# A hybrid attention stack on one core: what stays in the step, what moves behind it, and a centring in two rounded products

## The chip, the cores and the metric

The kernel runs on one core of one Trainium2 chip. The metric is device time in microseconds, the median of three runs of the same program. PE is TensorE, DVE is VectorE, ACT is ScalarE, POOL is GpSimd, SP is SyncE. PSUM is read by DVE and ACT and written by PE; POOL works on SBUF alone.

## The reference

The input x has 4 sequences of 512 tokens and 128 features. Four blocks follow each other, each with a residual:

```
x = x + attention_a(layernorm(x))          # 16 heads of 8, softmax, dense
x = x + ffn(layernorm(x))                  # two layers, below
x = x + attention_b(layernorm(x))          # linear attention, elu + 1
x = x + ffn(layernorm(x))                  # the same weights again
ffn layer: h = shift_token(x); q, k, v = h @ wqkv     # 8 heads of 64
           q, k = rotary_xpos(l2norm(q) * qs, l2norm(k) * ks)
           x = x + local_attention(q, k, v) @ wo      # windows of 64, one back
           h = layernorm(shift_token(x)) * lg + lb
           a, g = split(h @ w1 + b1); x = x + (a * gelu(g)) @ w2 + b2
```

`shift_token` delays the upper 64 features by one token. In the kernel's layout, features on partitions and tokens along the row, that is a copy of partitions 64 to 127 by one column. All is float32; large products are made from a value rounded to FP32R (`_h`, the high part) and what the rounding left (`_l`, the low part).

## The kernel before, in words

The program has two phases, `attention_a` and `stream`, both written with semaphores by hand. The change lies in `stream`. It walks over 64 tiles of 128 tokens: 2 calls of the ffn, 2 layers each, 4 sequences, 4 tiles to a sequence. Four tiles are a group (16 of them): what is done for a whole sequence is done once in a group.

Each engine has a list in `STEP` (L985): a stage, a lag in steps, and whose turn it is. In step s an engine runs the stages of its list in the order in which they stand there, each for tile s minus its lag. So an engine's order is fixed, and an instruction that waits holds up all that stands behind it. `of_tile` stages run in every step, `of_group` stages in every fourth, and `of_sequence` stages once for each sequence between the two calls, where attention b and two layer norms lie. Counting from the last tile of a group, the output product `wo` comes at lag 3, the MLP's centring at 4, `w1` at 5, `w2` at 6 on PE and its result on DVE at 7. So steps come in fours. I name them by their group work: step A has `wo` (and on DVE the result of the group before, `w2`), step B the MLP's centring and its variance, step C `w1` and the gelu, step D `w2`. Of a sequence between the calls, A has the norm b (`center_b`, `var_b`), B the latent and key products, C the context and token products, D the projection and the norm y (`center_y`, `var_y`).

In every step PE turns the weighed scores (`turn_p`, L1314), projects q, k and v (L1265 to L1267), turns q and k (L1276), multiplies by the values (`sums`, L1324), and makes the next scores (L1289, L1304). ACT squares and copies, takes the row norms (`norm`) and the exponentials (`soften`, L1499). DVE copies the turned scores (`PT`, L1644), sums and inverts them (`weigh`, L1661, L1663), does the rotary products (`rope`, L1616, L1620, L1627) and the maxima (`soften`, L1652). POOL multiplies the scores by the inverse sums (`weigh`, L1196), adds the rotary halves and scales them by the row norms (`scale`, L1185, L1190).

PSUM has 8 banks and PE takes them in turn: `take` gives the product number x bank x modulo 8, and waits until what read the product 8 before has gone through (`FREED`). So every bank that is read late stops PE, though the data of the product itself are there.

A layer norm has a product that takes off the mean (`center_*`, L1366), a square on ACT (L1537), a product with ones (`var_*`, L1372), Ln and Exp on ACT (L1544, L1547), and DVE's multiplication (stage `var_*`, L1676 to L1692). For the MLP (`center_mlp`) POOL first makes the shifted sequence in `mid` (stage `wo`, L1216 to L1220), and PE multiplies it in float32. After `w2`, DVE writes the high part `HH` of the next layer's input straight from PSUM in two halves (L1717) and then `Y` (L1721); POOL makes the low part `HL` (L1177, stage `w2`). Norm y does the same on DVE (L1689, L1692) and POOL (stage `var_y`). Layer 1 of a call has no such parts: there DVE writes only X (L1710), and POOL adds Y to X behind `mid` (L1224).

Of the kernel before, what the change touches and what calls it, by code (L numbers as in the profile page):

```python
# [7 lines left out]
F32 = mybir.dt.float32  # L8
# [971 lines left out]
def of_first(k):  # L980
# [5 lines left out]
    "PE": [("turn_p", 3, of_tile), ("turn_p_2", 3, of_tile),  # L986
# [4 lines left out]
           ("center_y", 10, of_sequence), ("keys_b", 8, of_sequence), ("tokens_b", 9, of_sequence), ("scores", 1, of_tile),  # L991
           ("var_mlp", 4, of_group), ("var_a", 3, of_first), ("var_b", 7, of_sequence),
           ("var_y", 10, of_sequence), ("w2", 6, of_group), ("wo", 3, of_group), ("store", 7, of_end)],
    "ACT": [("squares", 0, of_tile), ("latent", 8, of_sequence), ("features_b", 10, of_sequence), ("values", 0, of_tile),
            ("turn", 1, of_tile), ("sums", 3, of_tile), ("features_a", 1, of_first),
            ("center_mlp", 4, of_group), ("center_a", 3, of_first), ("center_b", 7, of_sequence),
            ("center_y", 10, of_sequence), ("split", SEQS, of_tile), ("w1", 5, of_group), ("keys_b", 8, of_sequence),
            ("norm", 0, of_tile), ("var_mlp", 4, of_group), ("var_a", 3, of_first), ("var_b", 7, of_sequence),
            ("var_y", 10, of_sequence), ("soften", 1, of_tile), ("split_w1", 4, of_first), ("store", 7, of_end)],
    "DVE": [("lead", 0, of_lead), ("turn_p", 3, of_tile), ("var_mlp", 5, of_group), ("var_a", 4, of_first),  # L1000
            ("var_b", 8, of_sequence), ("var_y", 11, of_sequence), ("w2", 7, of_group),
            ("weigh", 2, of_tile), ("latent", 8, of_sequence), ("rope", 0, of_tile),
            ("project_a", 2, of_first), ("context", 9, of_sequence), ("project_b", 10, of_sequence),
            ("w1", 5, of_group), ("keys_b", 8, of_sequence), ("soften", 1, of_tile),
            ("tokens_b", 9, of_sequence), ("wo", 3, of_group)],
    "POOL": [("split_w1", 5, of_first), ("lead", 0, of_lead), ("split", SEQS, of_tile), ("weigh", 2, of_tile), ("scale", 0, of_tile), ("w2", 6, of_group),
             ("wo", 3, of_group), ("latent", 8, of_sequence), ("var_y", 10, of_sequence)],
# [32 lines left out]
def stream(nc, a, g, out):  # L1040
# [53 lines left out]
    with ExitStack() as ctx:  # L1094
# [21 lines left out]
        mid = sb("mid", [P, T])  # L1116
# [16 lines left out]
        OF = g.raw[:, 2 * T:3 * T]  # L1133
# [5 lines left out]
        with block:  # L1139
# [25 lines left out]
            def _(pool):  # L1165
# [6 lines left out]
                nc.gpsimd.memset(mid[64:P, 0:1], 0.0).then_inc(s("mid_zero"), 1)  # L1172
                pool.wait_ge(s("mid_zero"), 1)
# [7 lines left out]
                for stage, i in engine_plan("POOL"):  # L1181
# [29 lines left out]
                    elif stage == "wo":  # L1211
# [4 lines left out]
                        nc.gpsimd.tensor_copy(mid[0:64, :], Y[0:64, n, :]).then_inc(s("shifted_mid"), 1)  # L1216
                        pool.wait_ge(s("shifted_mid"), 2 * i + 1)
                        nc.gpsimd.tensor_copy(mid[64:P, 1:T], Y[64:P, n, 0:T - 1]).then_inc(s("shifted_mid"), 1)
                        if i:
                            nc.gpsimd.memset(mid[64:P, 0:1], 0.0).then_inc(s("mid_zero"), 1)  # L1220
                            pool.wait_ge(s("mid_zero"), i + 1)
                        pool.wait_ge(s("shifted_mid"), 2 * i + 2)
# [3 lines left out]
                    elif stage == "w2" and not last_layer(i):  # L1226
                        pool.wait_ge(s("y_new"), i + 1)
                        call = i // (SEQS * LAYERS)
                        low_part(i % SEQS, "shifted", 2 * (SEQS * call + i % SEQS))
                    elif stage == "latent":  # L1230
                        pool.wait_ge(s("q_exp"), i + 1)
                        pool.wait_ge(s("q_pos"), i + 1)
                        nc.gpsimd.tensor_tensor(QB[:, :], QB[:, :], NEG[:, :], ALU.add).then_inc(s("q_ready"), 1)
                    elif stage == "var_y":
                        n = i
                        pool.wait_ge(s("ln_used"), number["y", n] + 1)
                        low_part(n, "again_shifted", 2 * n)

            @block.tensor
            def _(pe):  # L1240
# [89 lines left out]
                for stage, i in engine_plan("PE"):  # L1330
# [20 lines left out]
                    elif stage[:7] == "center_":  # L1351
                        use, j = stage[7:], i
                        if use == "mlp":
                            pe.wait_ge(s("shifted_mid"), 2 * j + 2)
                            pe.wait_ge(s("mid_zero"), j + 1)
                            x = mid[:, :]
# [9 lines left out]
                        nc.tensor.matmul(take("center", number[use, j]), cst("center"), x, start=True, stop=True)\  # L1366
                          .then_inc(s("center"), 1)
# [73 lines left out]
                    elif stage == "project_a":  # L1441
                        pe.wait_ge(s("o_ready_a"), 1)
                        nc.tensor.matmul(take("project_a", i), g.wpa[:, :], NEG[:, :], start=True, stop=True)\
# [13 lines left out]
            def _(act):  # L1457
                for stage, i in engine_plan("ACT"):
# [102 lines left out]
                    elif stage == "split_w1":  # L1561
                        nc.scalar.activation(w1_h[:, :, :], w1, ACT.Copy).then_inc(s("w1_high"), 1)
                    elif stage == "latent":
# [3 lines left out]
                        else:  # L1567
                            act.wait_ge(s("ones_b"), 2)
                        nc.scalar.activation(LAT[0:32, :], psum[0:32, bank("latent", i), :], ACT.Identity,
                                             bias=g.bd_b[:, 0:1]).then_inc(s("latent_ready"), 1)  # L1570
                        act.wait_ge(s("q_neg"), i + 1)
# [28 lines left out]
            def _(dve):  # L1600
# [6 lines left out]
                for stage, i in engine_plan("DVE"):  # L1607
# [61 lines left out]
                    elif stage[:4] == "var_":  # L1669
# [4 lines left out]
                        if use == "mlp":  # L1674
# [126 lines left out]
```

## Time and profile before

| | us |
|---|---|
| median of 3 runs | 1014.11 (1013.69 to 1014.61) |
| the profiled execution | 1009.97 |
| its span, first to last instruction | 1007.9 |
| PE busy | 916.4 (91%) |
| DVE busy | 796.0 (79%) |
| ACT busy | 701.6 (70%) |
| POOL busy | 509.8 (51%) |

The span begins with attention a; the stream's first scores come at some 257 us and its last store at the end. Busy PE is not PE at its peak, since the ends of matmuls are modelled, so waits of PE are read from the timeline, where the number in brackets is the idle time just before an instruction and what ended it.

### The profile page before, as it was taken

How to read it: one execution, taken by the hardware profiler on the slowest of the kernel's cores; microseconds unless marked ns; L12 is line 12 of the kernel's file. 1: busy time of each engine (PE TensorE's matmuls, PEld its weight loads, DVE VectorE, ACT ScalarE, POOL GpSimd, SP SyncE). 2: the span in 40 equal slices, each digit the busy share in tenths (PEclk: the TensorE clock that was granted, in tenths of full speed). 3: DMA queues.
4: the chain of work that ended last, by engine and by line, in shares of the span. 5: the costliest groups of instructions: out<-in, count | busy, mean ns of one | idle time of the engine just before them, and what ended most of it. 6: DMA issues, size and time to landing. Idle time of an engine off the chain costs nothing.

```text
span 1007.9 us, 22385 instructions
## 1 busy us (share of the span) xinstructions
PE 916.4 (91%) x8584; PEld 569.8 (57%) x8584; DVE 796.0 (79%) x1170; ACT 701.6 (70%) x1500; POOL 509.8 (51%) x336
## 2 busy tenths in 40 slices
PE   8999999999778999999988887888979999999985
PEld 4333333333556776776756564565747677677753
DVE  6887878885678899999977687756778999998862
ACT  3577777778576696887866575665758688787753
POOL 2110113123577668578664545544456857867730
PEclk9999999999989999999999999999999999999997
DMA  2211000000201001101000000000000110101100
GB/s 81 65 39 33 2 1 2 3 1 2 70 16 28 22 17 33 29 17 33 18 22 17 12 17 22 17 12 16 12 23 17 33 28 17 33 17 38 35 10 21
DMA packets 23205, 23.46 MB, mean 23 GB/s; under 512 B 8530, under 2 KB 14972, under 8 KB 23100
## 3 DMA queue, kind: packets, MB, share of 16 engines
q1 hardware_dynamic: 23100, 22.04, 8.8%
q8 instruction: 69, 1.13, 0.5%
q14 instruction: 36, 0.29, 0.1%
HBM read 6.16 MB, written 1.05 MB: 7 GB/s over the span
## 4 chain that ended last, share of the span: by engine, by line
PE 50%; DVE 14%; issue 5%; POOL 3%; ACT 3%; DVEq 0%; ACTq 0%; POOLq 0%
PE psum L1348 5%; PE psum L1324 5%; PE psum L1304 5%; PE psum L1392 4%; PE psum L1276 4%; PE psum L1314 3%; PE psum L1265 3%; DVE f_PT L1644 3%; PE psum L1366 3%; PE psum L1383 2%; PE psum L1267 2%; PE psum L1266 2%; PE psum L1384 2%; PE psum L1385 2%; PE psum L1372 2%
## 5 line engine op out<-in xcount | busy, mean ns | idle before, releaser
L876 DVE TENSOR_REDUCE a_M<-psum 128x2 f32<-128x1024 f32 x128 | 155.3, 1220 | 33.4 <-PE psum L650 32.7
L1196 POOL TENSOR_TENSOR f_PW<-f_PW,f_RD 128x1024 f32<-128x1024 f32 x64 | 121.4, 1898 | 102.9 <-DVE f_RD L1663 101.1
L1185 POOL TENSOR_TENSOR A<-A,BS 128x1024 f32<-128x1024 f32 x62 | 146.8, 2368 | 33.2 <-DVE BS L1620 33.2
L1190 POOL TENSOR_TENSOR A<-A,RN 128x1024 f32<-128x1024 f32 x62 | 118.1, 1905 | 64.3 <-ACT RN L1514 58.7
L773 ACT ACTIVATE a_PT<-psum 128x1024 f32<-128x1024 f32 x128 | 128.9, 1020 | 23.8 <-PE psum L660 23.7
L1499 ACT ACTIVATE f_PW<-psum,f_NM 128x128 f32<-128x128 f32 x512 | 138.4, 380 | 5.6 <-DVE f_NM L1652 5.5
L1652 DVE TENSOR_REDUCE f_NM<-psum 128x4 f32<-128x512 f32 x128 | 82.1, 683 | 43.3 <-PE psum L1304 43.3
L1644 DVE COPY f_PT<-psum 128x512 f32<-128x512 f32 x128 | 82.3, 683 | 29.0 <-PE psum L1314 28.9
L1465 ACT ACTIVATE SQ<-psum 128x512 f32<-128x512 f32 x124 | 72.5, 622 | 39.5 <-PE psum L1267 35.7
L1661 DVE TENSOR_REDUCE f_RD<-f_PW 128x8 f32<-128x1024 f32 x64 | 77.5, 1211 | 9.4 <-ACT f_PW L1499 9.4
L1620 DVE TENSOR_TENSOR BS<-psum,sin 128x512 f32<-128x512 f32 x124 | 84.2, 679 | 0.0
L1616 DVE TENSOR_TENSOR A<-psum,cos 128x512 f32<-128x512 f32 x124 | 82.7, 667 | 0.0
L571 PE MATMUL psum<-a_PT,a_VA 128*12 128x256 f32 x1024 | 79.6, 383 | 0.6 <-ACT a_PT L773 0.6
L1314 PEld LDWEIGHTS psum<-const,f_PW 128*128 128x128 f32 x512 | 59.2, 142 | 34.2 <-issue 24.4
L1314 PE MATMUL psum<-const,f_PW 128*128 128x128 f32 x512 | 68.7, 278 | 7.0 <-POOL f_PW L1196 7.0
L1627 DVE TENSOR_REDUCE SS<-SQ 128x16 f32<-128x1024 f32 x62 | 74.8, 1207 | 0.0
L1276 PE MATMUL psum<-const,A 128*128 128x128 f32 x512 | 68.0, 276 | 6.7 <-POOL A L1190 4.7
L1304 PE MATMUL psum<-f_KT,f_QT 64*64 64x128 f32 x2048 | 70.5, 278 | 2.9 <-ACT f_KT L1489 2.9
L1324 PE MATMUL psum<-f_PT,f_VS 128*64 128x64 f32 x1024 | 67.0, 229 | 4.5 <-DVE f_PT L1644 2.7
L1276 PEld LDWEIGHTS psum<-const,A 128*128 128x128 f32 x512 | 59.1, 142 | 20.3 <-POOL A L1190 10.7
L1304 PEld LDWEIGHTS psum<-f_KT,f_QT 64*64 64x64 f32 x2048 | 61.9, 138 | 10.8 <-ACT f_KT L1489 6.8
L1324 PE MATMUL psum<-f_PT,V 128*64 128x64 f32 x1024 | 64.1, 223 | 0.0
(216 smaller groups left out, 2007.5 us busy)
## 6 DMA issues: line engine op xcount, KB each, us to landing
f_VS<-V SPq DMA_DIRECT2D x112, 128.0 KB, 2.3
raw<-L_ffn_wqkv_dram SPq DMA_DIRECT2D x2, 768.0 KB, 4.6
a_XT<-L_attn_a_x_dram SPq DMA_DIRECT2D x4, 256.0 KB, 2.8
out_dram<-raw SPq DMA_DIRECT2D x4, 256.0 KB, 2.3
gates<-L_ffn_w_dram SPq DMA_DIRECT2D x2, 341.0 KB
tables<-const_dram SPq DMA_DIRECT2D x1, 512.0 KB, 3.8
wo<-L_ffn_wo_dram SPq DMA_DIRECT2D x2, 256.0 KB
const<-const_dram SPq DMA_DIRECT2D x1, 264.0 KB, 3.1
```

The costliest lines, as they stand in the source:

```text
L773: nc.scalar.activation(PT[:, i % 4, :, :], psum[:, pair("by_key", i), :], ACT.Exp, scale=float(DA) ** -0.5).then_inc(s("exped"), 1)
L876: nc.vector.tensor_reduce(M[:, quads % 2, t, 2 * j:2 * j + 2], psum[:, pair("scores", i), :], AX_X, ALU.max).then_inc(s("maxed"), 1)
L1185: nc.gpsimd.tensor_tensor(A[:, k % 2, :, :], A[:, k % 2, :, :], BS[:, k % 2, :, :], ALU.add)\
L1190: nc.gpsimd.tensor_tensor(x, x, RN[:, k % 2, :, None].to_broadcast([P, 2 * HW, DW]), ALU.mult)\
L1196: nc.gpsimd.tensor_tensor(x, x, RD[:, k % 2, :, None].to_broadcast([P, 2 * PAIRS, P]), ALU.mult)\
L1276: last = nc.tensor.transpose(dst[:, P * c:P * c + P], A[:, k % 2, w, P * c:P * c + P], g.ident)
L1304: last = nc.tensor.matmul(dst[j][WIN * w:WIN * w + WIN, P * c:P * c + P].rearrange("p (s x) -> p s x", s=2), QT[rows, k % 2, c, WIN * w:WI ...
L1314: last = nc.tensor.transpose(dst[:, P * c:P * c + P], PW[:, u % 4, c, :], g.ident)
L1324: last = nc.tensor.matmul(dst[DW * j:DW * j + DW, c, WIN * w:WIN * w + WIN], values[:, k % 4, 2 * c + j, :], PT[:, (2 * k + j) % 4, c, WIN ...
L1499: last = nc.scalar.activation(PW[:, u % 4, c, :], psum[:, bank("scores", u), P * c:P * c + P], ACT.Exp, bias=NM[:, u % 4, c:c + 1])
L1620: nc.vector.tensor_tensor(BS[:, k % 2, w, :].rearrange("p (h s d) -> p h s d", s=2, d=DW // 2), x.rearrange("p (h s d) -> p h s d", s=2, d ...
L1644: nc.vector.tensor_copy(PT[:, u % 4, :, :], psum[:, bank("turn_p", u), :].rearrange("p (c x) -> p c x", c=PAIRS))\
```

## The change

All of it is in `stream`.

- Order. PE: `center_y` goes from ahead of the scores to behind `w2`, at the end of step D; `var_y` goes from the end of step D into the next step (A), behind the two `turn_p`. ACT: the squares and roots of norm y move likewise; the exponential of attention b's queries becomes a stage of its own (`latent_exp`) behind `w1`. DVE: the stages `var_mlp` and `var_b`, which stood at the head of the next step, go to the end of the step in which the variance is made, ahead of `wo`; what frees no bank there is split off: `rest_mlp` (L1680, L1683) stays in step C behind `turn_p`, and `rest_w2` and `rest_y` copy HH from Y in SBUF, behind `rope` and behind `soften`. `latent` goes behind `rope`. POOL: `weigh` and `scale` now stand first; `split`, `split_w1` and `lead` last; the low part after `w2` is made at lag 7 (step A, ahead of the stage `wo`) and not at lag 6 (step D); that of norm y at lag 11.
- The MLP's centring. POOL makes the high and the low part of the shifted sequence, and PE multiplies each by a rounded centring matrix `centre`, in place of one float32 product of `mid`.
- A buffer: OF of its own, which attention a's last features use too.

```diff
 "PE":
-  ("turn_p", 3), ("turn_p_2", 3), ("project", 0) ...
+  ("turn_p", 3), ("turn_p_2", 3), ("var_y", 11), ("project", 0) ...
-  ("center_b", 7), ("center_y", 10), ("keys_b", 8) ... ("var_b", 7), ("var_y", 10), ("w2", 6), ("wo", 3)
+  ("center_b", 7), ("keys_b", 8) ... ("var_b", 7), ("w2", 6), ("center_y", 10), ("wo", 3)
 "ACT":
+  ("var_y", 11) first; ("latent_exp", 8) behind ("w1", 5); ("center_y", 10) just ahead of ("soften", 1)
 "DVE":
-  lead, turn_p 3, var_mlp 5, var_a 4, var_b 8, var_y 11, w2 7, weigh, latent 8, rope,
-  project_a, context 9, project_b 10, w1, keys_b 8, soften, tokens_b 9, wo 3
+  lead, turn_p 3, var_y 11, rest_mlp 5, w2 7, weigh, rope, rest_w2 7,
+  project_a, context 9, project_b 10, latent 8, w1, keys_b 8, soften, rest_y 11,
+  tokens_b 9, var_mlp 4, var_a 3, var_b 7, wo 3
 "POOL":
-  split_w1 5, lead, split, weigh 2, scale 0, w2 6, wo 3, latent 8, var_y 10
+  weigh 2, scale 0, w2 7, wo 3, latent 8, var_y 11, lead, split_w1 5, split
```
```diff
 POOL, stage wo:
-  tensor_copy(mid[0:64, :], Y[0:64, n, :])
-  tensor_copy(mid[64:P, 1:T], Y[64:P, n, 0:T - 1])
-  memset(mid[64:P, 0:1], 0.0)
+  for half, (rows, to, of) in enumerate(SHIFTED):
+      tensor_copy(mid_h[rows, to], Y[rows, n, of])
+  tensor_copy(mid_h[64:P, 0:1], HH[64:P, n, 0:1]); tensor_copy(mid_l[64:P, 0:1], HL[64:P, n, 0:1])
+  for half, (rows, to, of) in enumerate(SHIFTED):
+      tensor_tensor(mid_l[rows, to], Y[rows, n, of], mid_h[rows, to], subtract)
 PE, center_mlp:
-  matmul(dst, cst("center"), mid, start=True, stop=True)
+  matmul(dst, centre, mid_h, start=True, stop=False); matmul(dst, centre, mid_l, start=False, stop=True)
 DVE, w2 of layer 0:
-  for rows, to, of in SHIFTED: scalar_tensor_tensor(out=HH[rows, n, to], in0=psum ..., in1=Y ...)
   scalar_tensor_tensor(out=Y[:, n, :], in0=psum ..., in1=Y[:, n, :])
+ DVE, rest_w2 (and rest_y alike):
+  for rows, to, of in SHIFTED: tensor_copy(HH[rows, n, to], Y[rows, n, of])
 POOL, stage w2:
-  pool.wait_ge(s("y_new"), i + 1)
+  pool.wait_ge(s("high"), ...)       # rest_w2's two copies
```

## Rows read from the trace of the kernel before

**Rows 1.** Busy time by stretch: length, then engines with instructions, granted clock, DMA share, GB/s.

```profile
421.65:460.74 39.09, 38.39 (x410) 27.65 (x409) 36.09 (x54) 30.63 (x77) 28.17 (x18) 1.00 0.11 25
558.26:618.93 60.67, 51.71 (x451) 34.45 (x450) 43.22 (x70) 37.95 (x90) 30.76 (x19) 0.97 0.07 16
601.47:618.93 17.46, 14.42 (x113) 8.64 (x110) 10.99 (x20) 9.49 (x27) 8.05 (x4) 0.90 0.07 16
612.07:615.48 3.41, 3.41 (x39) 1.90 (x37) 0.00 (x0) 1.31 (x4) 0.92 (x2) 0.50 0.02 5
726.08:741.96 15.88, 12.85 (x113) 7.80 (x110) 10.99 (x20) 9.47 (x27) 8.05 (x4) 1.00 0.08 18
```

**Rows 2.** Timeline, PE in sequences: start, length, line, idle time before and its releaser.

```profile
611.54 0.73 PE L1366 MATMUL psum<-X,const 128*128 128x512 f32 x1 [2.97 <-DVE X L1778]
622.96 0.50 PE L1265 MATMUL psum<-w_h,HH 128*128 128x512 f32 x1 [2.29 <-DVE Y L1692]
635.90 0.50 PE L1265 MATMUL psum<-w_h,HH 128*128 128x512 f32 x1 [1.00 <-DVE Y L1692]
642.39 1.10 PE L1366 MATMUL psum<-f_mid,const 128*128 128x512 f32 x2 [0.83 <-DVE BS L1620]
650.38 0.48 PE L1265 MATMUL psum<-w_h,HH 128*128 128x512 f32 x1 [1.69 <-DVE f_ln_squared L1676]
```

**Rows 3.** Timeline of a layer-0 group: PE, DVE and POOL from step A on.

```profile
421.65 1.04 PE L1314 MATMUL psum<-const,f_PW 128*128 128x128 f32 x8
423.49 1.52 DVE L1717 SCALAR_TENSOR_TENSOR HH<-psum,vecs,Y 64x512 fp32r<-64x512 f32 x2
428.47 3.67 PE L1348 MATMUL psum<-f_OT,wo 128*128 128x512 f32 x8 [0.21 <-DVE BS L1620]
428.84 0.68 DVE L1620 TENSOR_TENSOR BS<-psum,sin 128x512 f32<-128x512 f32 x1
435.81 0.10 POOL L1220 MEMSET f_mid<- 64x1 f32 x1
436.98 1.13 PE L1366 MATMUL psum<-f_mid,const 128*128 128x512 f32 x2
443.65 1.03 PE L1276 MATMUL psum<-const,A 128*128 128x128 f32 x8
```

**Rows 4.** Groups by line and form, POOL: busy us, mean ns of one, idle before.

```profile
L1185 POOL TENSOR_TENSOR A<-A,BS 128x1024 f32<-128x1024 f32 x62 | 146.8, 2368 | 33.2 <-DVE BS L1620 33.2
L1196 POOL TENSOR_TENSOR f_PW<-f_PW,f_RD 128x1024 f32<-128x1024 f32 x64 | 121.4, 1898 | 102.9 <-DVE f_RD L1663 101.1
L1190 POOL TENSOR_TENSOR A<-A,RN 128x1024 f32<-128x1024 f32 x62 | 118.1, 1905 | 64.3 <-ACT RN L1514 58.7
L1177 POOL TENSOR_TENSOR HL<-Y,HH 64x512 fp32r<-64x512 f32 x13 | 16.6, 1274 | 42.4 <-DVE Y L1721 22.3 <-DVE Y L1692 19.2 <-DVE HH L1604 0.8
L1177 POOL TENSOR_TENSOR HL<-Y,HH 64x511 fp32r<-64x511 f32 x13 | 14.2, 1089 | 1.0
L1218 POOL COPY f_mid<-Y 64x511 f32<-64x511 f32 x16 | 9.8, 612 | 1.0
```

**Rows 5.** The chain in order of time: start, us, what; PE's issue of one product.

```profile
437.05 1.05 PE psum L1366 x2
446.19 0.23 PE psum L1384
```

**Rows 6.** DVE's SBUF copies at L1604 (min/median/max ns), and POOL then.

```profile
L1604 DVE CAST HH<-Y x2: 425/1240/2056, 319.5 to 321.5; 64x512 fp32r<-64x512 f32 x1, 64x511 fp32r<-64x511 f32 x1
319.33 1.91 POOL L1190 TENSOR_TENSOR A<-A,RN 128x1024 f32<-128x1024 f32 x1
```

**Rows 7.** The stream's start: POOL's weight split ahead of weighing, and DVE.

```profile
302.19 0.20 DVE L1663 RECIPROCAL f_RD<-f_RD 128x8 f32<-128x8 f32 x1
306.17 1.26 POOL L1209 TENSOR_TENSOR f_qkv_l<-raw,f_qkv_h 128x512 fp32r<-128x512 f32 x1 [3.53 <-ACT f_qkv_h L1528]
```

**Rows 8.** The last group: PE's wait for the shifted sequence.

```profile
986.72 1.10 PE L1366 MATMUL psum<-f_mid,const 128*128 128x512 f32 x2 [1.77 <-POOL f_mid L1218]
```

More of the change, by code:

```diff
@@ L998 @@
             ("norm", 0, of_tile), ("var_mlp", 4, of_group), ("var_a", 3, of_first), ("var_b", 7, of_sequence),
[L999 to L1005, printed above, removed]
@@ L1006 @@
-    "POOL": [("split_w1", 5, of_first), ("lead", 0, of_lead), ("split", SEQS, of_tile), ("weigh", 2, of_tile), ("scale", 0, of_tile), ("w2", 6, of_group),
-             ("wo", 3, of_group), ("latent", 8, of_sequence), ("var_y", 10, of_sequence)],
+            ("center_y", 10, of_sequence), ("soften", 1, of_tile), ("split_w1", 4, of_first), ("store", 7, of_end)],
+    "DVE": [("lead", 0, of_lead), ("turn_p", 3, of_tile), ("var_y", 11, of_sequence), ("rest_mlp", 5, of_group),
+            ("w2", 7, of_group), ("weigh", 2, of_tile), ("rope", 0, of_tile), ("rest_w2", 7, of_group),
+            ("project_a", 2, of_first), ("context", 9, of_sequence), ("project_b", 10, of_sequence), ("latent", 8, of_sequence),
+            ("w1", 5, of_group), ("keys_b", 8, of_sequence), ("soften", 1, of_tile), ("rest_y", 11, of_sequence),
+            ("tokens_b", 9, of_sequence), ("var_mlp", 4, of_group), ("var_a", 3, of_first),
+            ("var_b", 7, of_sequence), ("wo", 3, of_group)],
@@ L1008 @@
+    "POOL": [("weigh", 2, of_tile), ("scale", 0, of_tile), ("w2", 7, of_group),
+             ("wo", 3, of_group), ("latent", 8, of_sequence), ("var_y", 11, of_sequence), ("lead", 0, of_lead), ("split_w1", 5, of_first), ("split", SEQS, of_tile)],
     "SP": [("values", 0, of_tile), ("store", 7, of_end)],
@@ L1115, in stream @@
         w1_l = sb("w1_l", [P, LAYERS, 2 * HID], F32R)
-        mid = sb("mid", [P, T])
+        centre = sb("centre", [P, P], F32R)
         mid_h = sb("mid_h", [P, T], F32R)
@@ L1132, in stream @@
         OB = sb("OB", [P, 4, HA, DA])
-        OF = g.raw[:, 2 * T:3 * T]
+        OF = sb("OF", [P, T])
         OUT = g.raw[:, 0:8 * P].rearrange("p (b t d) -> p b t d", b=2, t=4)
@@ L1442, in _ @@
                         pe.wait_ge(s("o_ready_a"), 1)
-                        nc.tensor.matmul(take("project_a", i), g.wpa[:, :], NEG[:, :], start=True, stop=True)\
+                        nc.tensor.matmul(take("project_a", i), g.wpa[:, :], OF[:, :], start=True, stop=True)\
                           .then_inc(s("project_a"), 1)
@@ L1723, in _ @@
                               .then_inc(s("y_new"), 1)
+                    elif stage == "rest_w2":
+                        if not last_layer(i):
+                            dve.wait_ge(s("y_new"), i + 1)
+                            for rows, to, of in SHIFTED:
+                                nc.vector.tensor_copy(HH[rows, i % SEQS, to], Y[rows, i % SEQS, of])\
+                                  .then_inc(s("high"), 1)
                     elif stage == "latent":
```

83 lines of the change are left out of this document (44 added, 39 removed).

## The prediction

> **What bounds the kernel now.** The page's slices show PE at eight or nine tenths all through, so I looked first for where PE is not busy, by stretches [rows 1]. Two kinds of steps stand out. A layer-0 group, four steps without work of the sequences, takes 39.09 us, of which PE is busy 38.39 and DVE 36.09; POOL has 28.17. There PE is the bound, with DVE close behind, and less than 1 us of waiting is to be had. Four steps in which a sequence passes between the calls take 60.67, of which PE is busy 51.71: 9 us of waiting in each. There are four sequences. Step D alone takes 17.46 with 14.42 of PE.
>
> The timeline says what PE waits for in such four steps [rows 2]: 2.97 us for X, ahead of `center_y` in D; 2.29 for Y in A, because the bank of that centring comes free only when DVE has made two halves of HH and then Y; 1.00 in B for the Y of norm b; 0.83 in B at the MLP's centring, for a bank that `rope` frees late; 1.69 in C for the bank of the MLP's centring. That is 8.8 of the 9. All are of one kind: an instruction in PE's or DVE's fixed order stands ahead of others that could run. The granted clock adds to the first: for 3.41 us behind the wait it is 0.50, the 1.2 GHz level, and a D without such a stretch takes 15.88, not 17.46 [rows 1].
>
> **Norm y and the sequences: 32 us off.** In D, X is ready at 611.5. Behind the scores and `w2`, PE comes to `center_y` later than that, so the 2.97 goes, and with it the half clock, some 1.6. Against that, the scores must now wait for `rope` to free their second bank, about 1.2 us after PE gets there, and `var_y` (about 1, as one float32 product of 512 columns) goes to A. I get 13.1 for D, 4.4 off in the three that show the low clock, 2.8 in the fourth: 16. In A, Y needs no HH ahead of it any more, so the 2.29 goes; but ACT's square now waits for the late `center_y` and holds up the exponentials behind it, so Ln and Exp of norm y come about 4 us into A, and the result of `w2` behind Y at 5.7, where PE wants its bank at 3.9. With `var_y` itself A stays at 14.2 to 14.4: 0, and 1 off for the one A that had a low clock. In B, the 1.00 and the 0.83 go, since `var_b` stands ahead of `wo` and `latent` behind `rope`; with 0.5 of the cheaper centring and what the earlier `rope` frees I take 2.9 in each, 12 to 13. In C, the MLP's multiplication now stands ahead of the copies PT, which takes 0.6 of the 1.69. Four times that is 2.4. The sum is 16 + 1 + 12.6 + 2.4 = 32. From below, if only D gains, it is 16; from above, all of the 8.8, the clock and the cheaper centring, it is 4 x 11 = 44. I take 32, since each term goes by a named wait.
>
> **The start: 5 us off.** In each of three steps POOL waits for ACT's rounding of a weight block and only then weighs: the inverse sums were ready at 302.4, the split ran from 306.17 to 307.4, and weighing began behind it [rows 7]. Behind `scale`, the split delays nobody in its own step, but it and `split_w1` push the next step's weighing. Following the three steps through, PE's turn in step 8 comes 5 us earlier. The bounds are the three splits alone, 3 x 1.26 = 3.8, and three times this wait of 5.0, 15.
>
> **The MLP's centring: dearer on POOL than it is cheaper on PE.** On PE a float32 product of 512 columns is two passes, 1.05 with the last; an FP32R product issues in 0.23 [rows 5]. Two of those for 1.05 save about 0.5. On POOL `mid` was two copies and a memset, 1.3. Now there are two rounding copies (0.6 each), two of one column (0.1 each, as the memset [rows 3]) and two subtractions like those of HL (1.27 and 1.09 [rows 4]): 3.8, and with six waits on its own results 4.1. So 2.8 more in each of 16 groups, and PE waits for it. Whether that shows depends on where POOL stands, so I follow one layer-0 group from A's first transposition, 421.65 [rows 3].
>
> In A, HH's two halves (1.5) leave DVE ahead of `weigh`, so `rope` ends its last product not at 7.9 but at 6.4. PE's `wo`, which waited for it, comes 0.56 earlier, and with it the unhindered centring of B: 436.98 - 421.65 - 0.56 = 14.8. POOL, though, has a row of work that no longer has a gap. It adds the halves from 6.45 on: 2.37, then 0.15 and 1.9 for the scaling, to 10.9 [rows 4]. Then comes the low part after `w2`, which used to run in the wait at the step's head and now stands between: 2.43, to 13.4, or to 13.9 since HH's copies come late (below). Then the parts of the shifted sequence, 4.1, to 17.5 or 18.0. So PE waits 3 us at the centring, where it waited for nothing. From 18.0 POOL goes on with B's weighing, addition and scaling, 1.9 + 2.37 + 1.9 and 0.25 between, to 24.4, and C's turn of q and k needs that. It stood at 443.65 - 421.65 = 22.0. The group ends 2.4 later than before, in spite of the cheaper centring and of A's 0.56.
>
> There are five such groups, 12. In the two where the new group is of layer 1, POOL's addition to X (1.28) lies in the chain too: 3.5 each, 7. In the step where the last sequence's norm y meets this, both low parts are in the chain: 3. In two groups of layer 1 without HL I get 0.8 each, 1.6. In the sequences' steps PE has the latent products ahead of the centring, and POOL comes in time: 0. The sum is 24. From below it is 0, if POOL's work can hide after all; from above the whole 2.8 + 2.43 in each of ten, 52. I take 24, since the chain is the sum of durations that hardly vary.
>
> At the end nothing hides it: PE waits 1.77 for the shifted sequence even now [rows 8], so the last group costs 2.8 - 0.5 = 2.3 more. A PE that waits 3 us may run at 1.2 GHz for a stretch, as in D; there that cost 1.6 in three of four cases. Here most of it lies beside POOL's chain; I add 2.5 in all, from bounds of 0 and 8 x 1.6 = 13.
>
> **The copies of HH.** They read SBUF now and no longer PSUM. Where POOL stood still such a copy took 0.43; the one that met POOL's scaling, which began 0.13 before it, took 2.06 and ended behind it [rows 6]. So `rest_w2`, which comes just while POOL adds and scales, costs DVE between 0.85 and some 4 us. In a layer-0 group DVE then waits beside POOL, and PE waits longer for POOL in any case: 0 to 0.5, in the 18.0 above.
> The Trainium skill (SBUF — State Buffer, Who interferes with whom) has a rule that speaks against this move: the port pair that VectorE and GpSimd share is an exclusive lock, held for a whole instruction by whichever starts first, for copies in a two-port mode too. The row agrees for one direction. By the rule DVE can also come first, and then POOL's chain grows by up to 0.85 in each group with a low part: that would make 1013 of the time, and it is in the second rival.
>
> **The sum.** The terms are -32 - 5 + 24 + 2.3 + 2.5 = -8.2. The profiled execution's 1009.97 becomes 1001.8. The median of the runs lies 4.1 above that execution, and I carry that over: 1014.1 - 8.2 = 1005.9, so 1006. The other edits, OF's buffer, `project_a`, the rounding of `centre`, are single instructions beside other work: 0.
>
> **The rivals.**
> 1. POOL's chain is hidden: PE's order or DVE's delays leave POOL the time, and its 24 + 2.5 fall to some 5. Then 1014.1 - 32 - 5 + 2.3 + 5 = 984; with half of it, 995. For it: POOL is busy only 28 of 39 us in a group [rows 1]. Against it: its work is in the middle, and both ends of the chain are fixed.
> 2. POOL's chain is dearer, and the kernel slower. Place: step A and B of the eight groups where a low part comes ahead of the centring. Price: 2.4 to 3.5, and 1.6 for the clock, and 0.85 where DVE's copies go first: 5 to 6 in each, 45 in all. It decides from 4.4 in each, where 8 x 4.4 + 2.3 is the 37 that the rest saves. At 45 the time is 1014.1 - 37 + 45 + 2.3 = 1024. For it: a wait of 2.97 already brings the low clock.
> 3. The sequences gain in D alone: the waits in A, B and C come back under other names, since DVE is busy 43.2 of 60.67 and its order has few gaps. Then 1014.1 - 16 - 5 + 26.5 + 2.3 = 1022. Against it: each of those waits has its own cause, which the change takes away.
> 4. Gain and loss even out: 1014.
>
> **How the numbers follow.** What tells two runs of this kernel apart is about 0.2%, 2 us. My forecast, 1006 with its own range of 998 to 1012, has 0.48. Rival 1 has 0.22, rival 2 0.13, rival 3 0.08, rival 4 0.09. Faster is the forecast and rival 1, 0.70; the same is rival 4, 0.09; slower is rivals 2 and 3, 0.21. The range of 8 in 10 takes in half of rival 1 and the near ends of the slower ones: 989 to 1020.
>
> **What would show it.** Right: in the changed kernel's timeline PE waits 2 to 3 us for POOL's subtraction at the MLP's centring in layer-0 groups, and a group takes 41 to 42 us; step D takes 13 and B 11 to 12; four steps of a sequence take 52 to 54. POOL's work in a group [rows 1] rises by 2.8. Wrong: groups of 39 us or less (rival 1), a clock of 0.5 in each group (rival 2), or sequences of 57 and more (rival 3).

## The result and the profile after: slower by 0.9%, since the centring now waits for two engines

| | before | after |
|---|---|---|
| median of five runs, us | 1014.11 (1009.55 to 1014.87) | 1022.64 (1020.00 to 1023.77) |
| ratio to before | | 1.0088 [1.0061, 1.0114] |
| profiled execution; its span | 1009.97; 1007.9 | 1022.71; 1020.7 |
| PE, DVE, ACT, POOL busy in the span | 916.4, 796.0, 701.6, 509.8 | 923.1, 816.6, 696.4, 553.7 |

The page of the changed kernel, the busy time of each engine:

```profile
span 1020.7 us, 22419 instructions
PE 923.1 (90%) x8584; PEld 572.4 (56%) x8584; DVE 816.6 (80%) x1170; ACT 696.4 (68%) x1501; POOL 553.7 (54%) x384
```

The page names no culprit: POOL has 44 us more to do, DVE 21, PE 7. Where the time went is seen by steps, numbered as in `STEP`: step 3 is the first in which PE turns weighed scores, and step 18 the A of the layer-0 group below. The table takes the start of each step from PE's first transposition of the weighed scores and adds up the lengths of the steps. It compares one profiled execution of each kernel.

| stretch | before | after | difference | forecast |
|---|---|---|---|---|
| up to step 9 (the start) | 343.4 | 340.7 | -2.7 | -5 |
| steps 10 to 25, four groups in which POOL makes HL | 156.9 | 173.5 | +16.6 | |
| steps 26 to 41, the four sequences | 241.6 | 212.2 | -29.4 | -32 |
| steps 42 to 57, four more of them | 161.3 | 179.9 | +18.6 | |
| steps 58 to 65, two groups without HL | 73.6 | 78.7 | +5.2 | |
| all groups together | 391.8 | 432.2 | +40.4 | +24 +2.5 |
| from step 66 to the end | | | +4.5 | +2.3 |

The windows of the changed kernel that answer to rows 1: two layer-0 groups that follow each other (with and without a stretch at half clock), that stretch, a step D, a sequence's four steps (columns as there).

```profile
384.51:428.26 43.75, 40.46 (x409) 28.32 (x408) 38.21 (x54) 30.14 (x77) 30.89 (x21) 0.96 0.10 22
428.26:470.47 42.21, 38.98 (x410) 27.38 (x409) 38.21 (x54) 30.14 (x77) 30.95 (x21) 1.00 0.10 23
403.70:407.11 3.41, 3.41 (x32) 1.94 (x25) 1.29 (x2) 0.90 (x4) 3.27 (x3) 0.50 0.00 0
605.79:618.94 13.15, 11.79 (x111) 7.57 (x108) 10.90 (x20) 6.65 (x19) 8.05 (x4) 1.00 0.09 21
565.07:618.94 53.87, 49.48 (x451) 33.79 (x450) 44.53 (x70) 37.70 (x89) 33.65 (x22) 1.00 0.08 18
```

A sequence now takes 53.87 and not 60.67, at the full clock throughout. But a layer-0 group takes 42.21 or 43.75 and not 39.09. Eight groups have POOL's HL ahead of the centring as these two do; in two of them POOL also adds to X, and in one the last sequence's norm y comes in. The timeline of the group without half clock, where A begins at 428.26 and B at 438.01 (start, length, line; in brackets the idle time before and its releaser):

```profile
434.65 2.35 POOL L1183 TENSOR_TENSOR A<-A,BS 128x1024 f32<-128x1024 f32 x1 [0.47 <-DVE BS L1630]
435.62 3.71 DVE L1733 CAST HH<-Y 64x512 fp32r<-64x512 f32 x2
437.14 1.90 POOL L1188 TENSOR_TENSOR A<-A,RN 128x1024 f32<-128x1024 f32 x1
439.41 2.46 POOL L1175 TENSOR_TENSOR HL<-Y,HH 64x512 fp32r<-64x512 f32 x2 [0.36 <-DVE HH L1733]
440.68 0.69 DVE L1677 TENSOR_TENSOR Y<-Y,psum 128x512 f32<-128x512 f32 x1
441.94 1.28 POOL L1215 CAST f_mid_h<-Y 64x512 fp32r<-64x512 f32 x2
443.79 2.43 POOL L1222 TENSOR_TENSOR f_mid_l<-Y,f_mid_h 64x512 fp32r<-64x512 f32 x2
446.32 0.47 PE L1371 MATMUL psum<-f_mid_h,f_centre 128*128 128x512 f32 x1 [2.27 <-issue]
452.61 1.09 PE L1278 MATMUL psum<-const,A 128*128 128x128 f32 x8
```

Read it from the last but one line upwards. PE waits 2.27 us at the centring; the profile writes "issue", but POOL's second subtraction ends at 446.22, 0.1 before. POOL goes from 437.14 to there almost without a gap: the scaling, HL, the two casts, two copies of one column, the two subtractions. And DVE stands in its own copies of HH for 3.71 us, beside POOL's addition and scaling; the maxima come only behind them, and then Y (L1677), from which POOL makes the centring's parts (the high and the low part of the shifted sequence).

The first three of these lines are step C of the same group: two lines of DVE stand in a new order, and PE waits for a bank behind them. The fourth is the last group, where PE's wait of rows 8 has grown by 2.96:

```profile
450.71 0.75 DVE L1686 SCALAR_TENSOR_TENSOR f_ln_squared<-psum,vecs,f_LR 128x512 f32<-128x512 f32 x1 [1.11 <-ACT f_LR L1555]
451.38 1.28 DVE L1654 COPY f_PT<-psum 128x512 f32<-128x512 f32 x2
457.63 0.50 PE L1391 MATMUL psum<-f_mid_h,f_w_h 128*128 128x512 f32 x1 [0.23 <-DVE BS L1630]
997.94 0.76 PE L1371 MATMUL psum<-f_mid_h,f_centre 128*128 128x512 f32 x1 [4.73 <-issue]
```

PE's waits of the changed kernel, by line (total, times, longest); the second is the one that rows 2 show with 1.69 in step C of a sequence:

```profile
PE psum L1371 <- issue: 21.8, 9, 4.7
PE psum L1267 <- DVE f_ln_squared L1686: 5.8, 4, 1.4
PE psum L1391 <- DVE BS L1630: 4.8, 17, 0.8
```

### The profile page after: what moved, and what is told of

Its sections match the earlier page's. It is cut to its first block, busy times and chain, and to the rows that moved or that the text cites. A ratio compares the mean times of both kernels' runs of the same rounds, so it can differ in the third digit from the quotient of the medians.

```text
span 1020.7 us, 22419 instructions
## 1 busy us (share of the span) xinstructions
PE 923.1 (90%) x8584; PEld 572.4 (56%) x8584; DVE 816.6 (80%) x1170; ACT 696.4 (68%) x1501; POOL 553.7 (54%) x384
## 4 chain that ended last, share of the span: by engine, by line
PE 37%; DVE 15%; ACT 8%; issue 7%; POOL 6%; DVEq 0%; ACTq 0%; POOLq 0%
PE psum L1306 5%; PE psum L1400 4%; ACT f_PW L1507 4%; PE psum L1326 4%; PE psum L1278 3%; DVE BS L1630 3%; PE psum L1316 2%; PE psum L1380 2%; DVE A L1626 2%; DVE HH L1733 2%; PE psum L1391 2%; DVE f_RD L1671 2%; PE psum L1350 2%; PE psum L1291 2%; POOL A L1183 2%
## 5 line engine op out<-in xcount | busy, mean ns | idle before, releaser
L773 ACT ACTIVATE a_PT<-psum 128x1024 f32<-128x1024 f32 x128 | 129.0, 1020 | 23.9 <-PE psum L660 23.7
L1188 POOL TENSOR_TENSOR A<-A,RN 128x1024 f32<-128x1024 f32 x62 | 118.0, 1903 | 43.5 <-ACT RN L1522 36.2
L1662 DVE TENSOR_REDUCE f_NM<-psum 128x4 f32<-128x512 f32 x128 | 82.2, 684 | 35.5 <-PE psum L1306 35.2
L1278 PE MATMUL psum<-const,A 128*128 128x128 f32 x512 | 70.1, 277 | 23.3 <-POOL A L1188 10.5
L1278 PEld LDWEIGHTS psum<-const,A 128*128 128x128 f32 x512 | 56.7, 140 | 43.9 <-POOL A L1188 18.6
L1473 ACT ACTIVATE SQ<-psum 128x512 f32<-128x512 f32 x124 | 71.5, 631 | 11.1 <-PE psum L1269 9.1
L1306 PE MATMUL psum<-f_KT,f_QT 64*64 64x128 f32 x2048 | 74.3, 288 | 2.5 <-ACT f_KT L1497 2.5
L1306 PEld LDWEIGHTS psum<-f_KT,f_QT 64*64 64x64 f32 x2048 | 65.1, 144 | 10.6 <-ACT f_KT L1497 6.5
```

Of the source, the lines that this page charges most:

```text
L773: nc.scalar.activation(PT[:, i % 4, :, :], psum[:, pair("by_key", i), :], ACT.Exp, scale=float(DA) ** -0.5).then_inc(s("exped"), 1)
L1188: nc.gpsimd.tensor_tensor(x, x, RN[:, k % 2, :, None].to_broadcast([P, 2 * HW, DW]), ALU.mult)\
L1278: last = nc.tensor.transpose(dst[:, P * c:P * c + P], A[:, k % 2, w, P * c:P * c + P], g.ident)
L1306: last = nc.tensor.matmul(dst[j][WIN * w:WIN * w + WIN, P * c:P * c + P].rearrange("p (s x) -> p s x", s=2), QT[rows, k % 2, c, WIN * w:WI ...
```

## The experiments

The theory after the comparison: the order gains what it was forecast to gain; the split centring loses it again, because in each group its parts end later than PE comes to it. I call a gate what must be done before the centring can begin. Rivals: the order itself costs the groups their time (VectorE's blocked copies, its moved `var_mlp`); or the half clock behind the wait does. All are variants of the changed kernel, but `split_only`, which is one of the kernel before. The stretches are those of the table by steps, in us of the profiled execution; B and C are medians of steps 10 to 25. Each ratio is to runs of the kernel before from the same round. The edits are shown shortened.

| run | ratio to before [95%] | 10-25 | 26-41 | 42-57 | 58-65 | B | C |
|---|---|---|---|---|---|---|---|
| before | 1 | 156.9 | 241.6 | 161.3 | 73.6 | 8.24 | 11.17 |
| after | 1.0088 [1.0061, 1.0114] | 173.5 | 212.2 | 179.9 | 78.7 | 12.62 | 11.99 |
| order_only | 0.9797 [0.9752, 0.9842] | 164.5 | 213.1 | 169.6 | 75.1 | 9.39 | 12.61 |
| split_only | 1.0425 [1.0372, 1.0477] | 168.4 | 252.3 | 171.0 | 79.9 | 10.57 | 11.72 |
| low_later | 1.0009 [0.9983, 1.0036] | 169.2 | 212.2 | 174.7 | 78.8 | 10.80 | 12.04 |
| filler | 1.0028 [1.0007, 1.0049] | 170.1 | 212.2 | 176.2 | 78.7 | 11.14 | 12.02 |
| act_copies | 1.0085 [1.0051, 1.0119] | 171.5 | 212.2 | 180.5 | 77.3 | 11.96 | 12.03 |
| both_gates | 0.9797 [0.9762, 0.9833] | 158.4 | 212.2 | 164.2 | 78.8 | 8.19 | 12.01 |
| var_head | 1.0066 [1.0046, 1.0087] | 171.3 | 212.7 | 177.3 | 78.8 | 12.44 | 11.60 |
| order_var_head | 0.9792 [0.9735, 0.9849] | 161.0 | 214.1 | 166.5 | 73.6 | 9.39 | 11.72 |
| all_three | 0.9802 [0.9776, 0.9829] | 157.6 | 212.6 | 164.2 | 78.7 | 8.18 | 11.80 |
| order_var_act | 0.9647 [0.9621, 0.9673] | 155.9 | 214.2 | 161.5 | 73.6 | 8.24 | 11.29 |

### The two halves of the change

`order_only`: the new order; the centring, and the buffer of OF, as before.

```diff
 POOL, stage wo:
-  mid_h: two rounding copies and one column; mid_l: one column and two subtractions
+  mid: two copies and a memset
 PE, center_mlp:
-  matmul(dst, centre, mid_h, stop=False); matmul(dst, centre, mid_l, start=False)
+  matmul(dst, cst("center"), mid)
```

> The changed order of the engines with the float32 centring of before (POOL makes mid in two copies and a memset); OF and the last features of attention a are as before. Theory: in the changed kernel POOL's low part and the four copies and two subtractions of the centring stand in one chain ahead of it, which ends 17.96 us after step A begins. Without the subtractions it ends at 13.9 + 1.3 = 15.2, PE's centring comes at 14.8, so PE waits 0.5 and not 2.3 to 2.5, its clock stays up, and step B takes 8.5 to 9 and not 12.6: some 3.7 off in each of eight groups, the end 4 off, the sequences 2 longer: about 988 us. Step C stays near 12.0 if DVE's order sets it, and falls to 11.2 if POOL's chain sets it. Rival, the order itself loses (HH copied in SBUF blocks DVE for 3.7 us, the MLP's multiplication stands ahead of PT): B stays over 11 and the time over 1012.

Measured: 992.19 us; B is 9.39, more than the 8.5 to 9 expected, and C 12.61, over the 12.0 expected if DVE's order sets it. `split_only` is the other half, the same lines with the signs turned round, in the kernel before:

> The kernel before with the centring in two products alone. Theory: POOL's scaling in step A ends 13.0 us after the step's start, the parts take 4.3, so the centring waits from 15.3 to 17.3; weighing, adding and scaling behind it bring C's turn of q and k to 23.8 where it was 22.0. A group takes 1.8 longer, 3.3 with a low clock, with POOL's addition to X 1.3 more; eight to eleven groups and the end (2.3): 1030 to 1045 us. Rival, the order is what loses: the two products save 0.5 a group, and the time is at most 1014.

Measured: 1055.24 us, beyond the 1030 to 1045 expected, since the sequences lose too. So the order alone is worth 2.0%, and the split centring alone costs 4.2% in the old order and, from 0.9797 to 1.0088, 2.9% in the new one, some 29 us. It has not been a gain in either. In the old order the sequences take longer by it (252.3 for 241.6); in the new order they do not (212.2 with the split, 213.1 without). But `order_only` is not free of loss either: its four groups take 164.5 where the kernel before has 156.9. B has 1.1 too much, C 1.4. In B, with no wait at the centring, the same copies of HH stand ahead of the maxima as in the changed kernel:

```profile
426.87 3.71 DVE L1724 CAST HH<-Y 64x512 fp32r<-64x512 f32 x2
430.61 1.29 DVE L1653 TENSOR_REDUCE f_NM<-psum 128x4 f32<-128x512 f32 x2
432.63 0.63 PE L1276 MATMUL psum<-const,A 128*128 128x128 f32 x4 [0.24 <-ACT f_PW L1499]
433.57 0.66 PE L1276 MATMUL psum<-const,A 128*128 128x128 f32 x4 [0.31 <-ACT f_PW L1499]
```

### What the wait's half clock costs

`filler`: PE is given two float32 products ahead of the wait, whose result is overwritten, in the eight groups.

```diff
 PE, center_mlp, in eight groups:
+  for _ in range(2): matmul(dst, cst("ones"), cos)
   pe.wait_ge(s("mid_high"), 3 * j + 3)
```

> The changed kernel; in eight groups PE makes two more float32 products of 512 columns into the centring's own bank (the centring overwrites them) where it would wait for POOL, so that it stands still for 0.5 us and not 2.3. If the low clock behind the wait costs time of its own, B falls from 12.6 to 11.1 in the seven groups that show 0.50, and the time to about 1012. If the clock's part lies beside POOL's chain, as the prediction put it, the time stays at 1020 to 1023 or rises.

Measured: 1015.39 us. Timeline of PE at the centring, and the window of the group:

```profile
443.95 1.98 PE L1371 MATMUL psum<-cos,const 128*128 128x512 f32 x4
446.33 0.47 PE L1376 MATMUL psum<-f_mid_h,f_centre 128*128 128x512 f32 x1 [0.40 <-POOL f_mid_l L1222]
```
```profile
428.24:470.52 42.28, 40.96 (x413) 28.05 (x412) 38.19 (x54) 30.12 (x77) 30.95 (x21) 1.00 0.10 23
```

The centring comes 18.09 us into A, as in the changed kernel (18.06), but the granted clock stays at 1.00, in all eight groups, where it fell to 0.50 in seven. The medians differ by 7.3 us, and steps 10 to 57 are 7.1 shorter. So work that is thrown away bought 7 us. In four groups B is 1.4 to 1.5 shorter than in the changed kernel and C is not longer for it (11.99 and 12.02): there the half clock was not hidden beside POOL's chain. In the two groups in which POOL also adds to X it was hidden for the larger part: B is 1.2 and 1.3 shorter, but C 0.7 and 1.0 longer, and PE waits for POOL there, in the changed kernel not:

```profile
496.15 1.09 PE L1278 MATMUL psum<-const,A 128*128 128x128 f32 x8 [1.22 <-POOL A L1188]
```

### What holds the centring's parts

`low_later`: HL leaves POOL's chain, two steps later.

```diff
 "POOL":
-  ("weigh", 2), ("scale", 0), ("w2", 7) ...
+  ("weigh", 2), ("scale", 0), ("w2", 9) ...
```

> The changed kernel with one lag: POOL makes the low part after w2 at lag 9 (step C), and no longer ahead of the centring's parts in step A. Theory: the parts end at 11.0 + 4.3 = 15.3 us into A and B, PE waits 0.5, no low clock, B takes 8 to 8.5 and not 12.6; the low part fits into C's wait of POOL. Eight groups times 4: about 992 us. Rival, DVE is held by the copies of HH (3.7 us beside POOL, unchanged here) or by its new order: B stays at 11 or more, the time over 1012.

Measured: 1012.64 us; far from what was expected, since PE's wait only went from 2.27 to 1.78. The half clock came in three of the eight groups, though PE's wait was 1.77 or 1.78 in seven of them alike. Timeline, A from 425.83:

```profile
433.19 3.71 DVE L1733 CAST HH<-Y 64x512 fp32r<-64x512 f32 x2
438.25 0.69 DVE L1677 TENSOR_TENSOR Y<-Y,psum 128x512 f32<-128x512 f32 x1
439.00 1.28 POOL L1215 CAST f_mid_h<-Y 64x512 fp32r<-64x512 f32 x2 [2.39 <-DVE Y L1677]
443.40 0.47 PE L1371 MATMUL psum<-f_mid_h,f_centre 128*128 128x512 f32 x1 [1.78 <-issue]
```

POOL is free early now and stands 2.39 us for Y, which stands on DVE behind the copies of HH. The 2.46 us of HL were one gate of two. `act_copies` opens the other one alone:

```diff
 "DVE":  - ("rest_w2", 7) behind ("rope", 0)
 "ACT":  + ("rest_w2", 7) behind ("sums", 3)
 DVE, rest_w2:
-  tensor_copy(HH[rows, n, to], Y[rows, n, of])
+  scalar.activation(HH[rows, n, to], Y[rows, n, of], Copy)
```

> The changed kernel with one thing moved: the two shifted copies that fill HH (64x512 each), on VectorE in the changed kernel, are made by ScalarE behind its stage 'sums', so that the 3.71 us which the two take on VectorE beside GpSimd's work are gone from VectorE; GpSimd's queue is as in the changed kernel. In the run low_later, where GpSimd's HL subtraction was out of the way, PE still waited 1.98 to 2.00 us for the centring, with GpSimd idle for 2.39 us until VectorE's Y (L1677), which stood behind these copies. Theory (two gates side by side: VectorE's blocked copies hold y_mid, GpSimd's own chain of scale, HL and parts ends as late): opening this gate alone gains as little as opening the other did; the parts still end 17.4 to 17.7 us into step A, PE waits 1.7 to 2.0 us instead of 2.3 to 2.5, the low clock stays in most groups, 1012 to 1019 us. Rival (VectorE's copies are the gate by themselves): no wait at the centring, step B at 9.4 us or less instead of 12.6, 992 to 1000 us.

Measured: 1020.47 us, no better than the changed kernel. (The wait that the expectation gives for `low_later` as 1.98 to 2.00 is 1.78 in the timeline above.) Timeline, A from 426.86:

```profile
436.82 0.69 DVE L1683 TENSOR_TENSOR Y<-Y,psum 128x512 f32<-128x512 f32 x1 [1.33 <-PE psum L1350]
437.61 2.46 POOL L1175 TENSOR_TENSOR HL<-Y,HH 64x512 fp32r<-64x512 f32 x2
440.14 1.28 POOL L1215 CAST f_mid_h<-Y 64x512 fp32r<-64x512 f32 x2
444.53 0.47 PE L1371 MATMUL psum<-f_mid_h,f_centre 128*128 128x512 f32 x1 [2.84 <-issue]
```

Y is there 9.96 us into A and not 12.42, but POOL's chain ends as late as it did, less 0.4: behind its scaling, HL and the parts alone fill the time. PE comes to the centring earlier, waits longer, and in four groups the half clock lasts 6.8 us. That put the time beyond the end of what was expected. `both_gates` has both edits:

> The changed kernel with both edits: HH's copies on ScalarE (as act_copies) and GpSimd's HL subtraction two steps later (as low_later). Theory (two gates side by side): with both open GpSimd goes from the scale's multiply, which ends 10.8 us into step A, or from y_mid, to the parts of 4.28 us, which then end at 15.1 to 15.7 us, where PE comes to the centring at 15.6: the wait is 0 to 0.2 us, no low clock in the groups, step B 9.2 to 9.6 us, step C still 12.0, 995 to 1001 us. Rival (the parts are gated by a third thing, or PE loses the same time to other waits): step B over 10.5 us, over 1008 us.

Measured: 992.11 us, less than the 995 to 1001 expected; B is 8.19. Timeline, A from 419.44, and the window of the group:

```profile
425.05 1.27 ACT L1573 ACTIVATE HH<-Y 64x512 fp32r<-64x512 f32 x2
430.17 1.29 POOL L1215 CAST f_mid_h<-Y 64x512 fp32r<-64x512 f32 x2
432.04 2.45 POOL L1222 TENSOR_TENSOR f_mid_l<-Y,f_mid_h 64x512 fp32r<-64x512 f32 x2
434.59 0.47 PE L1371 MATMUL psum<-f_mid_h,f_centre 128*128 128x512 f32 x1 [0.33 <-issue]
```
```profile
419.44:458.79 39.35, 38.63 (x409) 27.47 (x408) 34.51 (x52) 31.61 (x78) 30.84 (x21) 1.00 0.11 25
```

One edit gave 10 us, the other 2, both together 30 (by the ratios, each to the kernel before of its own round: 8, 0.3 and 30). That is what two gates side by side look like: each hides what the other is worth. HH's two copies, 3.71 us on DVE beside POOL's addition and scaling, take 1.27 on ACT. They also come 1.75 us earlier in A there, at the end of POOL's weighing and the start of its addition. None of the eight groups has a stretch at half clock any more.

### Step C, and the best version

`var_head` puts the MLP's multiplication on DVE back behind the step's copies PT.

```diff
 "DVE":
-  ... ("tokens_b", 9), ("var_mlp", 4), ("var_a", 3) ...
+  ("lead", 0), ("turn_p", 3), ("var_y", 11), ("var_mlp", 5), ("rest_mlp", 5) ...
```

> The changed kernel with VectorE's stage var_mlp put back to where the kernel before has it, behind the step's copies of turn_p instead of at the end of the step before; all else is as in the changed kernel, the wait at the centring too. Theory (step C's length of 12.0 us comes from VectorE's order: L1686 waits for LR ahead of the copies of PT, which makes RD and the rope late and with them w1's bank): step C 11.0 to 11.4 us, B as in the changed kernel (11.1 to 12.7), 8 groups times 0.8 = 6: 1014 to 1018 us. Rival (step C's length is set by GpSimd's late chain or by the low clock behind the centring): C stays at 11.8 to 12.1, 1020 to 1024 us.

Measured: 1018.58 us, just past the 1014 to 1018 expected. DVE's two lines in C, where the copies now come first and L1686 finds LR ready:

```profile
448.27 1.29 DVE L1654 COPY f_PT<-psum 128x512 f32<-128x512 f32 x2 [0.17 <-PE psum L1316]
449.47 0.74 DVE L1686 SCALAR_TENSOR_TENSOR f_ln_squared<-psum,vecs,f_LR 128x512 f32<-128x512 f32 x1
```

In the groups of steps 10 to 25, C went from 12.0 to between 11.2 and 11.8 (to 11.8 where the granted clock was at 1.00 throughout), so DVE's order is a part of C's new length, not all of it. The intervals of the two ratios overlap; the groups' lengths show the gain (353.4 to 348.6), of which some 1.5 may be the half clock, seen in six groups and not seven. The same edit in the new order with the old centring:

> The run order_only (the changed order, the centring as before in one float32 product) with VectorE's stage var_mlp put back behind the step's copies of turn_p. In order_only step C took 12.6 us in the groups, where the kernel before has 11.2. Theory (VectorE's order sets step C): C 11.1 to 11.5 us, about 8 times 1.2 = 10 us less than order_only's 992: 979 to 986 us. Rival (C is set elsewhere, by the copies that fill HH or by GpSimd): C stays over 12.2 us, 989 to 993 us.

Measured: 989.12 us, 985.6 in the profiled execution; C 11.72 for 12.61: 0.9 of the 1.4 that C had lost, short of the 11.1 to 11.5 expected. Its four runs lie between 985.58 and 996.58, and by the ratios it cannot be told from `order_only`; the steps tell them apart. The last two versions put together what helped. `all_three` is the three edits in the changed kernel:

> The changed kernel with three edits together: HH's copies on ScalarE, GpSimd's HL subtraction two steps later (these two are both_gates, 992.1 us), and VectorE's var_mlp behind the step's copies of turn_p (var_head, where step C fell from 12.0 to 11.2 to 11.8 us). If the edits add up: B 8.2, C 11.2 to 11.8 us, 8 groups times 0.2 to 0.8: 985 to 991 us. If C is held by GpSimd's rope (3.4 us stall in the last C of layer 1) or by HH's copies instead, C stays at 12.0 and the time at 992.

Measured: 992.69 us, and not the 985 to 991 of edits that add up: C is 0.2 shorter, and against `both_gates` nothing can be told apart. `order_var_act` is `order_only` with HH's copies on ACT and the multiplication moved back:

> The changed order with the float32 centring of before (order_only, 992.2 us), with HH's copies on ScalarE and VectorE's var_mlp behind the copies of turn_p (order_var_head had 985.6 in its profiled execution: B 9.4, C 11.7). It differs from all_three in the centring and in where GpSimd makes HL. If VectorE's blocked copies are what is left in B (PE's 0.85 to 0.89 us ahead of L1276, the sums), B falls to 8.2 to 8.6 us and the time to 977 to 983 us; if C's 0.84 us ahead of L1265 go too, to 972. If the split centring has a worth of its own once nothing holds its parts, all_three is the faster of the two; if not, this is.

Measured: 977.07 us (974.29 to 979.63), 3.5% faster than the kernel before, at the low end of what was expected, and the best of all. Its layer-0 group is shorter than that of rows 1, and POOL has 2.6 us less in it than in `all_three`. The window of a group, first of `order_var_act`, then of `all_three`:

```profile
417.68:456.33 38.65, 38.44 (x410) 27.62 (x408) 34.75 (x52) 31.72 (x79) 28.24 (x18) 1.00 0.11 25
```
```profile
417.90:456.97 39.07, 38.31 (x410) 27.46 (x409) 35.22 (x52) 31.57 (x78) 30.81 (x21) 1.00 0.11 25
```

So even with both gates open the split centring is no gain on the whole. (The two runs also differ in the step in which POOL makes HL.) In this group `all_three` is 0.4 longer, and in all eight 4.4; in the two groups without HL 5.2 (78.7 and 73.6), where POOL's addition to X lies in the chain too. In the sequences it is 1.5 shorter (212.6 and 214.2). At the end PE waits longer for the parts, by the timelines of `all_three`:

```profile
965.72 0.77 PE L1371 MATMUL psum<-f_mid_h,f_centre 128*128 128x512 f32 x1 [4.73 <-issue]
```

and of `order_var_act`:

```profile
955.37 1.10 PE L1366 MATMUL psum<-f_mid,const 128*128 128x512 f32 x2 [1.77 <-POOL f_mid L1218]
```

The spans of the two profiled executions are 988.5 and 977.5, 11.0 apart; the groups, the sequences and this wait sum to just that. The medians are 15.6 apart, since `all_three`'s profiled execution, 990.65, is the fastest of its six runs and that of `order_var_act`, 979.63, the slowest of its six.

## Why the prediction was wrong

It gave 1006, from 989 to 1020; 1022.6 came. What happened is its rival 2, to which it gave 0.13: 35.2 us in the eight groups are 4.4 in each, the point from which it was to decide, and the saving came out smaller than the 37 counted there (32.1). The forecast saw the mechanism, PE waiting for POOL's subtraction at the centring, and its signs came: a wait of 2.27, groups of 42.21 where the clock stayed up, D 13.15, B 11.8, sequences of 53.87, POOL 2.78 busier in a group. The sign that it gave for rival 2, the clock of 0.5, came too. What failed is the price in the groups, 24 + 2.5 for 40.4: a delay in C that it put at nothing (about 6.5), the half clock that it took for mostly hidden (2.5 for 7.1), and the last two groups (1.6 for 5.2). The spans differ by +12.8 where the sum has -8.2, 21.0 apart. The medians are less far off, 16.6, since the profiled execution of before was 4.1 below its median and that of the changed kernel at its own.

- **Sequences: right.** -29.4 for -32. D is 13.15 in all four (13.1 forecast), together -15.6 for -16; A -1.2 for -1; B 11.8, together -12.3 for -12.6. Only C missed, -0.4 for -2.4: its wait ahead of L1267 stayed, 1.4 for 1.69.
- **Start: the mechanism right, one group not counted.** Steps 3 to 6 are 43.2 us before and 37.9 after, 5.2 less for 5. But step 7 has the first group's centring, and went from 9.45 to 12.06 by a wait of 2.25 for POOL's subtraction; there is no HL ahead of it yet, and `both_gates` did not cure this step (12.14). And the steps begin 0.9 later.
- **POOL's chain in A and B: right to a tenth.** The parts were to end 17.5 or 18.0 us into A, and ended at 446.22 - 428.26 = 17.96; the turn of q and k in C was to come at 24.4, and came at 452.61 - 428.26 = 24.35.
- **The clock: this step failed.** "Here most of it lies beside POOL's chain; I add 2.5 in all." The half clock came in seven of eight groups (in the one with the last sequence's norm y it began ahead of the centring, behind a wait of 1.43 for PT), at about 1.5 us in an ordinary group (43.75 - 42.21), and `filler`, which has none, is 7 us shorter. To be hidden, it would need PE to wait for POOL at C's turn of q and k. In the group without half clock PE comes there at 452.61 with no idle time shown, 0.06 behind the end of POOL's scaling (450.65 and 1.90 us): both are late alike, and whatever else delays PE is added. Only in the two groups where POOL also adds to X does PE have such a wait (1.22 and 1.50 in `filler`), and there `filler` gains just 0.5 and 0.3 in B and C, as the forecast had it. The missing slack could have been read from the forecast's own steps: from the centring at 14.8 to the turn at 22.0 - 0.56 - 0.5 = 20.9 PE needs 6.1; from 18.0 it is there at 24.1, and POOL at 24.4. Its upper bound, 13, had the loss; the value taken lay at the wrong end.
- **C: a term left out.** A group was to end 2.4 later. Without half clock it ended 42.21 - 39.09 = 3.1 later, and 0.8 of that is C, 11.99 for 11.17. The forecast followed `var_mlp` to the end of B on DVE, as a gain in the sequences, and did not ask what it stands in front of in a group: L1686 waits 1.11 for LR, with PT, the sums and the rotary products behind it. `var_head` gets back 0.2 to 0.8 of it in a step.
- **The copies of HH: wrong as a price.** "In a layer-0 group DVE then waits beside POOL, and PE waits longer for POOL in any case: 0 to 0.5." That held for the wait as it stood. They made PE itself 1.0 late at the centring, 15.79 us into A for the forecast's 14.8 (14.83 in `act_copies`), which POOL's chain hid. But `low_later` shows that the copies hold the centring for nearly as long as POOL's chain does, and in `order_only`, where POOL's chain is short, they still cost B 1.1, which `order_var_act` gets back (9.39 to 8.24).
- **The last groups and the end: too small.** Steps 58 to 65: 1.6 forecast, 5.2 measured: the first C (step 60) is 1.5 longer, the second (step 64) 3.9, the rest 0.2 shorter. In the second PE waits 3.26 for POOL's scaling, where it waited 0.92, and a half clock of 3.41 us follows; in `act_copies`, with the same wait and no half clock, this step is 1.5 shorter. The end: 2.3 forecast, 4.5 measured, of which 2.96 is PE's wait; for the rest I have no run, but the trace has the granted clock at 0.50 for 13.65 us from the end of that wait on, and, from 990.95 on, for 6.83 in the kernel before.
- **Who goes first at the shared port.** The forecast left it open and put the price of DVE going first, 0.85 a group, into rival 2. It did not come: the scaling, L1188, took 1.90 us beside DVE's copies, as its like did before [rows 4], and each of the 16 copies took 1661 to 2020 ns. The rule that the forecast drew on (the Trainium skill, SBUF — State Buffer, Who interferes with whom), that whichever engine starts first holds the port pair for its whole instruction, agrees with the end of the pair of copies shown: 439.33, behind POOL's 439.04, and only then do DVE's maxima begin. In all eight pairs each copy ended 0.28 behind POOL's instruction. That a copy would come first and POOL be late, which the rule allows, none of these rows shows; the scaling shown began 0.14 ahead of the end of the first copy, and was no longer for it.

Of the 21.0 the eight groups make 10.3 (35.2 for 22.4 and 2.5; C about 6.5 and the clock about 4.6, with 0.8 the other way), the last two 3.6, the start 2.3, the sequences 2.6 and the end 2.2. The forecast also took 2 us for what tells two runs of this kernel apart; the runs of the kernel before in one later round lie between 1009.65 and 1020.69.

## What to carry over

When a step's input is made by a chain on another engine, look for a second chain that ends nearly as late, before a part of the first is moved away or added: here 10 us and 2 us, each alone, were 30 together. A reordering that helps one kind of step has to be followed through the other kinds, which are more numerous. And the half clock that came behind a wait was paid in full, 1.5 us, where PE had no slack at its next meeting with the engine that it waited for; where it had, 0.3 to 0.5 was left.

## What the runs showed of the hardware

The granted clock fell to 0.50 behind PE's waits at the centring, but the length of the wait did not settle it. Of the eight groups seven are alike in this wait (the eighth has the last sequence's norm y). In the changed kernel it is 2.25 to 2.27 us in all seven, and the half clock came in six of them, not in the one whose timeline is shown; in `var_head`, with 2.26 to 2.29, in five; in `act_copies`, with 2.78 to 2.85, in six; in `low_later`, with 1.77 or 1.78, and in `split_only`, with 1.91 to 1.96, in two each; in `filler` and `both_gates`, with 0.27 to 0.41, in none. What decides between equal waits is open. Two float32 products whose result nobody reads, put into the wait, kept the granted clock at 1.00 in all eight.

A rounding copy of half of Y in SBUF, 0.43 us on DVE alone [rows 6], took 1.66 beside POOL's addition and 2.02 beside its scaling in each of the eight groups. On ACT it took 0.61 to 0.63 in each of 16 cases, though POOL was at work for 0.3 to 0.5 of that. ACT was not tried beside the addition and scaling as a whole.
